# Graph values of a pair put on their diagonal by DMA; edge sums spread over feed-forward bodies; last pair with idle products and VectorE copies

## The chip, the cores and the metric

One core of one Trainium2 chip. The metric is the device time of the whole kernel in microseconds, the median of several runs: 608.84 us for the kernel before (3 runs, 607.85 to 609.2).

## What is computed

`x` has 32 sequences of 128 tokens with 128 features. Three things are done to it, in this order.

1. Attention block: layer norm, scale and shift from a condition vector, 16 heads of 64, output projection, gate, residual.
2. Feed-forward block: layer norm, scale and shift, 128 to 512, GELU, 512 to 128, gate, residual.
3. Graph block, over the 128 tokens (rows) with the first 20 tokens as keys and values. `adj` is an integer mask of 11 labels for each pair of tokens.

```
self = concat(v, q) @ W_self.T + b_self          # q is left out for rows of v that sum to 0
for d in (0, 1):                                 # two directions: adj and adj transposed
    A    = (adj or its transpose)[:, :, :20, :]
    aff  = heads(self @ Wq[d]) . heads(self[:, :20] @ Wk[d]) / sqrt(8)        # 16 heads of 8
    aff  = where(A.sum(-1) > 0, aff, -9e15) + A @ w_bias + b_bias
    w    = softmax(aff)                          # over the 20 keys
    out += heads(w @ self[:, :20], Wout[d]) + bout[d]
y = v + relu(self + out)
```

Output projection and weighting commute, so the kernel first makes `values = self[:, :20] @ Wout[d].T` (20 rows, 16 heads of 8, two directions) and then weights them.

## The kernel before, in words

The 32 sequences are 16 pairs (`PAIRS`), and each stage has one body a pair, written out for the first and last pairs and looped for the rest. All five engines run their own program and meet in semaphores; the order on each engine is the order in which its `body(s)` is written. Attention runs to about 392 us of the span, feed-forward to about 457, graph bodies to the end.

**Graph body `s`** (`graph_phase`) works on three pairs at once. For pair `s` TensorE turns the softmax weights (`turn_w`, L2070) and multiplies them with the values (`weights_v`, L2084); for pair `s+1` it makes the scores (`affinity`, L2056); for pair `s+2` it makes self features (`self_features`, L2007), turns them (`turn_self`, L2014), makes keys and queries (`keys`, L2022, whose moving operand is two runs of 20 columns; `queries`, L2031); for pair `s+3` it turns x (`turn_x`, L1999). A pair has two sequences, b = 0 and 1. TensorE's order in body `s` is:

turn_w(s,0), self_features(s+2), values(s,0), affinity(s+1,0), weights_v(s,0), turn_self(s+2), turn_w(s,1), turn_x(s+3), values(s,1), affinity(s+1,1), keys(s+2), queries(s+2), weights_v(s,1).

**Values.** 16 heads x 20 keys are 320 rows; they are split into 3 chunks of 120, 120 and 80 rows (`HC` = 6 heads, `KC` = 120 rows, `GCH` = 3). `weights_v` needs, for each chunk, a block-diagonal matrix `v_block`: head h's 20 rows hold values only in head h's 8 columns, and a ninth column of ones gives the sum of the weights. ScalarE's `copy_keys` (L2157) repeats the 20 key columns six times, so that `values` (L2044) makes 120 rows x 256 columns at once for one sequence, and VectorE's `save_v` (L2248) multiplies by a 0/1 mask `v_mask` into `v_block`. The PSUM bank (`vo_ps`) is used in turn by `values` and by the output of `weights_v`. `v_mask` is made by GpSimd at the start (L1865, L1873) and the columns of ones are set by four VectorE copies (L1885) in attention body 1 (`set_constants`).

**VectorE in body s:** bias, maximum of pair s b=1 (L2254, L2264); reciprocal and output of pair s-1 b=1 (L2275, L2280); save_v(s,0); scores minus maximum (L2268); save_self(s+2) (L2241); reciprocal and output of pair s b=0; bias, maximum of pair s+1 b=0; save_v(s,1); scores minus maximum of s+1. **ScalarE:** save_wT(s,0) (L2190, L2193), exponentials (s,1) (L2183), rectify, save_selfT(s+2) (L2150), save_wT(s,1), save_xT(s+3) (L2144), exponentials (s+1,0), save_k (L2172), save_q (L2163), copy_keys(s+2). **SP** issues the loads of x and of the q row for pair s+4 behind `self_saved` of pair s+2, the store of pair s-1, and a residual load (L1894 to L1908).

In the last body both `values` stand at its head (L2044), and 5 idle products with the identity (`multiply_identity`, L2093, `FILL` = 5, each two instructions) follow each `turn_w`.

**Feed-forward bodies** (3.6 us each): VectorE also does edge work there: `sum_labels` of the last edge block (L327) in body 3 and the three instructions of `make_bias` (L344, L346, L349) in body 10. The next pair's split (L1659) comes behind them and gates the next `hidden` products (L1490).

**Feed-forward tail:** before graph body 0, TensorE does keys and queries of pairs 0 and 1 between the last feed-forward products; ScalarE's gates (L1590) stand between the graph's copies.

## Time and profile before

| | us |
|---|---|
| median of 3 runs | 608.84 (607.85 to 609.2) |
| profiled execution | 608.95 |
| its span (first to last instruction) | 607.4 |
| granted TensorE clock | 0.998 of full speed |
| busy: TensorE / its weight loads | 594.2 / 538.0 |
| busy: VectorE / ScalarE / GpSimd | 514.0 / 466.5 / 291.1 |
| DMA | 32.55 MB, mean 54 GB/s |

The profiled execution lies 0.11 us above the median, and 1.55 us of it lie outside the span. An fp32 product is recorded as two instructions. Matmuls overlap with the weight load of the next one, so their busy times add up to more than the time they take; the chain of waits gives the time that a group really adds.

### The profile page before, as it was taken

What the parts mean: (1) busy time and instruction counts of PE and PEld (TensorE: products, weight loads), DVE (VectorE), ACT (ScalarE), POOL (GpSimd) and SP (SyncE); (2) the same over time, 40 slices, a digit from 0 to 9 for tenths busy, and PEclk for the clock granted to TensorE, in tenths of its full rate; (3) what the DMA queues carried; (4) which work ended last, traced back from release to release, by engine and by line L of the source; (5) the groups of instructions that cost most, each with busy time, mean ns of one, the idle gap of its engine ahead of it and who ended that gap; (6) DMA issues with size and microseconds to landing.
All of it is one profiled execution on the core that took longest, in us unless ns stands there. A gap on an engine that the chain in (4) does not pass through costs nothing.

```text
span 607.4 us, 17246 instructions
## 1 busy us (share of the span) xinstructions
PE 594.2 (98%) x5570; PEld 538.0 (89%) x5570; DVE 514.0 (85%) x1132; ACT 466.5 (77%) x1703; POOL 291.1 (48%) x355
## 2 busy tenths in 40 slices
PE   8999999999999999999999999999998999999996
PEld 8889999999999999999999999888887888888886
DVE  5899989888988988998998998888867878888876
ACT  4888887988889789789889879778776566566563
POOL 4445435435435435345354354556643554554551
PEclk9999999999999999999999999999999999999999
DMA  8210210210210210210201202133421212212101
GB/s 239 82 40 9 49 50 10 57 46 9 56 41 15 56 37 19 56 31 24 56 13 42 64 2 57 53 96 105 131 86 54 69 38 71 60 44 69 54 17 36
DMA packets 54678, 32.55 MB, mean 54 GB/s; under 512 B 15200, under 2 KB 52464, under 8 KB 54640
## 3 DMA queue, kind: packets, MB, share of 16 engines
q1 hardware_dynamic: 53008, 27.85, 16.9%
q0 software_dynamic: 1632, 4.21, 2.2%
q8 instruction: 21, 0.34, 0.2%
q14 instruction: 17, 0.14, 0.1%
HBM read 25.74 MB, written 6.31 MB: 53 GB/s over the span
## 4 chain that ended last, share of the span: by engine, by line
PE 88%; DVE 6%; ACT 3%; issue 1%; DMA 1%; POOL 0%; ACTq 0%; DVEq 0%; SPq 0%; POOLq 0%
PE banks L701 10%; PE banks L731 10%; PE banks L714 9%; PE banks L2084 7%; PE banks L669 5%; PE banks L673 5%; PE banks L670 5%; PE banks L2056 4%; PE banks L2070 3%; PE banks L685 2%; PE banks L754 2%; PE banks L1501 2%; PE banks L755 2%; PE banks L756 2%; PE banks L2044 2%; PE banks L2031 2%
## 5 line engine op out<-in xcount | busy, mean ns | idle before, releaser
L593 POOL TENSOR_TENSOR late_blocks<-late_blocks,p_rsum 128x512 f32<-128x512 f32 x96 | 99.0, 1052 | 156.9 <-DVE p_rsum L1076 156.9
L928 ACT ACTIVATE late_blocks<-banks,neg_max 128x128 f32<-128x128 f32 x384 | 137.1, 402 | 27.9 <-DVE neg_max L1070 27.9
L928 ACT ACTIVATION_READ_ACCUMULATOR late_blocks<-banks,neg_max 128x1 f32 x384 | 93.2, 243 | 0.0
L909 ACT ACTIVATE wide<-banks 128x512 f32<-128x512 f32 x124 | 75.6, 610 | 5.5 <-PE banks L673 4.4
L669 PE MATMUL banks<-xT_hi,w_qkv_hi 128*128 128x256 f32 x256 | 77.7, 304 | 0.0
L1070 DVE TENSOR_REDUCE neg_max<-banks 128x8 f32<-128x1024 f32 x64 | 76.5, 1195 | 1.3 <-PE banks L701 1.3
L673 PE MATMUL banks<-xT_hi,w_qkv_lo 128*128 128x256 f32 x256 | 72.2, 282 | 0.0
L670 PE MATMUL banks<-xT_lo,w_qkv_hi 128*128 128x256 f32 x256 | 71.9, 281 | 0.0
L701 PE MATMUL banks<-wide 64*128 64x128 f32 x1024 | 66.0, 278 | 0.2
L701 PEld LDWEIGHTS banks<-wide 64*128 64x128 f32 x1024 | 59.8, 188 | 6.1 <-issue 3.5
L928 ACT ACTIVATE third_p<-banks,neg_max 128x128 f32<-128x128 f32 x128 | 47.0, 387 | 20.0 <-DVE neg_max L1070 20.0
L2183 ACT ACTIVATE late_weights<-late_weights 128x640 f32<-128x640 f32 x32 | 23.6, 737 | 49.5 <-DVE late_weights L2268 49.5
L1944 POOL TENSOR_TENSOR late_blocks<-blockmask,g_kT 128x320 f32<-128x320 f32 x32 | 27.2, 870 | 57.4 <-ACT g_kT L2172 57.4
L714 PE MATMUL banks<-ident,late_blocks 128*128 128x128 f32 x384 | 50.8, 275 | 1.8 <-DVE late_weights L1083 1.2
L1094 DVE CAST oT_hi<-banks 128x512 fp32r<-128x512 f32 x62 | 42.4, 684 | 10.8 <-PE banks L731 10.6
L2084 PEld LDWEIGHTS banks<-g_v_block,g_wT 120*128 120x128 f32 (+1 forms) x384 | 46.4, 191 | 4.0 <-DVE g_v_block L2248 3.3
L669 PEld LDWEIGHTS banks<-xT_hi,w_qkv_hi 128*128 128x128 f32 x256 | 48.8, 191 | 1.1
L670 PEld LDWEIGHTS banks<-xT_lo,w_qkv_hi 128*128 128x128 f32 x256 | 48.9, 191 | 0.6
L673 PEld LDWEIGHTS banks<-xT_hi,w_qkv_lo 128*128 128x128 f32 x256 | 48.6, 190 | 0.1
L714 PEld LDWEIGHTS banks<-ident,late_blocks 128*128 128x128 f32 x384 | 42.7, 140 | 6.6 <-issue 2.2
L2084 PE MATMUL banks<-g_v_block,g_wT 120*128 120x54 f32 (+1 forms) x384 | 47.3, 274 | 0.5 <-DVE g_v_block L2248 0.5
L1099 DVE TENSOR_TENSOR oT_lo<-banks,oT_hi 128x512 fp32r<-128x512 f32 x64 | 43.9, 686 | 2.3 <-ACT oT_hi L1007 1.2
(172 smaller groups left out, 1700.7 us busy)
## 6 DMA issues: line engine op xcount, KB each, us to landing
early<-in_mask SPq DMA_DIRECT2D x16, 220.0 KB
early<-in_mask SPq DMA_DIRECT2D x80, 44.0 KB
x_in<-in_x SPq DMA_DIRECT2D x16, 128.0 KB, 2.2
...
```

The lines of the kernel that those rows point to most:

```text
L593: pool.tensor_tensor(p[:, heads, :], p[:, heads, :], p_rsum[:, b, heads].unsqueeze(2).broadcast_to([128, 4, T]), ALU.mult).then_inc(p_read ...
L669: pe.matmul(dst, g.wq_hi[:, cols], xT_hi[par][:], start=True, stop=False)
L670: pe.matmul(dst, g.wq_hi[:, cols], xT_lo[par][:], start=False, stop=False)
L673: last = pe.matmul(dst, g.wq_lo[:, cols], xT_hi[par][:], start=False, stop=True)
L701: last = pe.matmul(s_ps[b][:, e, j, :], qk[rows, c, 0, b, :], qk[rows, c, 1, b, :], start=True, stop=True)
L714: last = pe.transpose(work_ps[bank][:, m * T:m * T + T], p[:, 4 * grp + m, :], g.ident[:])
L731: last = pe.matmul(work_ps[bank][64 * e:64 * e + 64, j * T:j * T + T], v[:, b, head * DH:head * DH + DH], pT[b][:, 2 * j + e, :], start=Tr ...
L909: act.activation(qk_dst(name) if name[0] == "q" else v_dst(name), work_ps[bank], ACT.Copy).then_inc(bank_free[bank], 1)
L928: act.activation(p[:, m, :], s_ps[b][:, e, j, :], ACT.Exp, bias=neg_max[:, b, 4 * e + j:4 * e + j + 1], accum_out=p_sum[:, b, m:m + 1]).th ...
L1070: dve.tensor_reduce(out=neg_max[:, b, :].rearrange("p (e j) -> p e j", e=2), in_=s_ps[b], op=ALU.max, axis=AX.X, negate=True).then_inc(max ...
L1099: dve.tensor_tensor(oT_lo[:, 4 * half:4 * half + 4, b, :], src, oT_hi[:, 4 * half:4 * half + 4, b, :].bitcast(F32), ALU.subtract).then_inc ...
L2084: last = pe.matmul(out_ps[:, d, heads, :].rearrange("p h v -> p (h v)"), wT[0:rows, d, c, :], v_block[0:rows, s.par, b, d, heads, :].rearr ...
```

## The change

- **Values once a pair.** `values(s)` now has the 2 x 20 key columns as its stationary operand and makes 40 rows x 288 columns (`Wout` padded from 16 to 18 heads and laid out as 6 x 3). It stands for pair s+2, ahead of turn_x(s+3). ScalarE copies the keys (`kvT`, 128x40) ahead of the turned self features, and copies the values to `v_rows` (two copies of 40x144) behind save_xT(s+3); `copy_keys` and VectorE's `save_v` go.
- **Diagonal by DMA.** SP writes `v_rows` into the diagonal blocks of an image in DRAM (two transfers a pair, runs of 216 bytes), waits for them, and loads the image as `v_block` (one transfer, 311 KB). The images are cleared once in attention body 14 (two stores of 311 KB). `weights_v` waits for the load, for the output copy of the sequence before, and, for b=1, for ScalarE's copies of the values of pair s+2. Its moving operand is now six runs of 9 columns.
- **Constants.** GpSimd's mask goes. VectorE's four copies become two memsets, of 40x324 and 120x1296.
- **Edge steps.** `sum_labels` of the last block is halved over feed-forward bodies 2 and 3, the three steps of `make_bias` go to bodies 10, 11 and 12, one each.
- **Tail of feed-forward.** `values` of pairs 0 and 1 follow their `queries`; the output products of the last pair wait for the copy of the values of pair 0.
- **Last pair.** 7 idle products at the head of the last body in place of the two `values`; VectorE does the second half of the last `save_wT`.

The diff, cut:

```diff
@@ -1541,11 +1557,13 @@
         pe.wait_ge(x2_ready, PAIRS - 2)
         begin.keys(pair(0))
         begin.queries(pair(0))
+        begin.values(pair(0))
         output(pair(PAIRS - 2))
         begin.turn_x(pair(1))
         pe.wait_ge(g.edges_made, 2)
         begin.affinity(pair(0), 0)
         begin.self_features(pair(1))
+        begin.wait_values(2)
         output(pair(PAIRS - 1))
         begin.wait_keys(1)
         turn_back(pair(PAIRS - 2))
@@ -1555,6 +1573,7 @@
         begin.affinity(pair(0), 1)
         begin.keys(pair(1))
         begin.queries(pair(1))
+        begin.values(pair(1))
         pe.wait_ge(x2_ready, PAIRS)
 
...
             if more(s, 2):
                 normalise(step_from(s, 2))
             test_rows(step_from(s, -2))
-            if at(s, 3):
-                edges.parts["sum_labels"](dve, PAIRS - 1)
-            if at(s, PAIRS - 6):
-                edges.parts["make_bias"](dve)
+            for part in range(2):
+                if at(s, 2 + part):
+                    edges.parts["sum_last_labels"](dve, part)
+            for part in range(3):
+                if at(s, PAIRS - 6 + part):
+                    edges.parts["make_bias"](dve, part)
 
         if steps:
...
-                pool.affine_select(out=part, in_=part, compare_op=ALU.is_ge, fill=0.0, base=base,
-                                   pattern=[[step_h, heads], [0, GD]], channel_multiplier=mult
-                                   ).then_inc(mask_steps, 1)
-                steps += 1
-                pool.wait_ge(mask_steps, steps)
+    ROW = HC * VW
+    DIAGONAL = NG * ROW + VW
+    v_image = nc.dram_tensor("v_image", (2, 2, HC * DIAGONAL), F32, kind="Internal").ap()
+
+    def v_whole(n):
+
+        return v_image[n][:, 0:KC * ROW].rearrange("b (p e) -> p b e", e=ROW)
+
+    def v_diagonal(n, b):
+
+        blocks = v_image[n, b].rearrange("(s x) -> s x", x=DIAGONAL)[:, 0:NG * ROW]
+        return blocks.rearrange("s (m e) -> m s e", e=ROW)[:, :, 0:VW]
 
     def set_constants(dve):
         dve.wait_ge(g.kept_loaded, KEPT * 16)
-        dve.wait_ge(mask_steps, 1 + 2 * GCH)
-        for n in range(2):
-
-            for b in range(2):
-                dve.tensor_copy(v_block[:, n, b, :, :, GD],
-                                v_mask[:, :, 0].unsqueeze(1).broadcast_to([KC, 2, GH]))
+        dve.memset(v_rows[:], 1.0)
+        dve.memset(v_block[:], 0.0).then_inc(v_cleared, 1)
         dve.tensor_scalar(q_bias[:], g.gqk_b[:, 0:2], GSCALE, None, ALU.mult)
         dve.tensor_tensor(b_gsum[:], g.b_gout[:, 0:D], g.b_gout[:, D:2 * D], ALU.add).then_inc(b_gouts_added, 1)
         dve.wait_ge(b_gouts_added, 1)
         dve.tensor_tensor(b_gsum[:], b_gsum[:], g.b_self[:], ALU.add).then_inc(consts_set, 1)
 
+    def clear_images(sp):
+
+        sp.wait_ge(v_cleared, 1)
+        for n in range(2):
+            sp.dma_start(v_whole(n),
+                         v_block[:, n].rearrange("p b s d c v -> p b (s d c v)")).then_inc(v_image_cleared, 16)
+
     def sync(sp):
+        def move_values(s):
+
+            if at(s, 0):
+                sp.wait_ge(v_image_cleared, 2 * 16)
+            zero_wait(sp, v_loaded[s.par], s.half * 16)
+            sp.wait_ge(v_saved, s.n * 2 + 2)
+            for b in range(2):
+                sp.dma_start(v_diagonal(s.par, b),
+                             v_rows[b * NG:b * NG + NG].rearrange("p s d c v -> p s (d c v)")
+                             ).then_inc(v_stored[s.par], 16)
+            sp.wait_ge(v_stored[s.par], s.half * 32 + 32)
+
+            zero_wait(sp, out_full, unit_count(step_from(s, -2), 1))
+            sp.dma_start(v_block[:, s.par].rearrange("p b s d c v -> p b (s d c v)"),
+                         v_whole(s.par)).then_inc(v_loaded[s.par], 16)
+
         def load(s):
             sp.dma_start(x_in[:, s.par], g.x2_p[s.n]).then_inc(x_loaded[s.par], 16)
             sp.dma_start(q_row[:, s.par],
@@ -2032,16 +2070,11 @@
                                  selfT[:].rearrange("p b t -> p (b t)"), start=True, stop=True)
             last.then_inc(q_full, 1)
 
-        def values(s, b):
-            pe.wait_ge(kv6_ready, s.n + 1)
-
-            if at(s, PAIRS - 1) and b == 1:
-                pe.wait_ge(q_saved, PAIRS)
-            elif at(s, PAIRS - 1):
-                pe.wait_ge(shifted, unit_count(s, 0))
-            else:
-                zero_wait(pe, o_ready, unit_count(s, b) - 1)
-            pe.matmul(values_at(s, b).rearrange("p d h v -> p (d h v)"), kvT6[:, s.par, b].rearrange("p h m -> p (h m)"),
+        def values(s):
+
+            zero_wait(pe, o_ready, unit_count(step_from(s, -2), 0))
+            pe.wait_ge(kv_saved, s.n + 1)
+            pe.matmul(v_ps.rearrange("p d s c v -> p (d s c v)"), kvT[:].rearrange("p b m -> p (b m)"),
                       g.gout_w[:].rearrange("p d v -> p (d v)"), start=True, stop=True).then_inc(v_full, 1)
 
...
 
         def weights_v(s, b):
 
-            pe.wait_ge(v_saved, unit_count(s, b))
-            if at(s, PAIRS - 1):
-                pe.wait_ge(o_ready, unit_count(s, b) - 1)
+            if at(s, 0) and b == 0:
+                pe.wait_ge(v_saved, 4)
+            if b == 0:
+                pe.wait_ge(v_loaded[s.par], s.half * 16 + 16)
+            zero_wait(pe, o_ready, unit_count(s, b) - 1)
+            if b == 1 and more(s, 2):
+                pe.wait_ge(v_saved, s.n * 2 + 6)
             for d in range(2):
                 pe.wait_ge(wT_saved[d], unit_count(s, b))
                 for c in range(GCH):
                     rows = min(KC, HM - c * KC)
                     heads = slice(c * HC, c * HC + rows // NG)
...
+                pe.matmul(dst, g.ident[:], g.ident[:], start=True, stop=True)
 
         def body(s):
             here, nxt, second = more(s, 0), more(s, 1), more(s, 2)
 
             if at(s, PAIRS - 1):
-                values(s, 0)
-                values(s, 1)
+                multiply_identity(turns_ps[:, 0:T], FILL + 2)
             if here:
                 turn_w(s, 0)
             if at(s, PAIRS - 1):
-                multiply_identity()
+                multiply_identity(g.bank[0][:, 512:512 + T], FILL)
             if second:
                 self_features(step_from(s, 2))
-            if here and not at(s, PAIRS - 1):
-                values(s, 0)
             if nxt:
                 affinity(step_from(s, 1), 0)
             if here:
@@ -2116,11 +2148,11 @@
             if here:
                 turn_w(s, 1)
             if at(s, PAIRS - 1):
-                multiply_identity()
+                multiply_identity(g.bank[0][:, 512:512 + T], FILL)
+            if second:
+                values(step_from(s, 2))
             if more(s, 3):
                 turn_x(step_from(s, 3))
-            if here and not at(s, PAIRS - 1):
-                values(s, 1)
             if nxt:
                 affinity(step_from(s, 1), 1)
             if second:
@@ -2132,8 +2164,9 @@
         if steps:
             begin = Kept()
             begin.turn_x, begin.self_features, begin.turn_self = turn_x, self_features, turn_self
-            begin.keys, begin.queries, begin.affinity = keys, queries, affinity
+            begin.keys, begin.queries, begin.values, begin.affinity = keys, queries, values, affinity
             begin.wait_keys = lambda count: pe.wait_ge(k_saved, count)
+            begin.wait_values = lambda count: pe.wait_ge(v_saved, count)
...
-            zero_wait(act, kv6_ready, s.n)
+            act.activation(kvT[:], turns_ps[:, 0:2 * T].rearrange("p (b t) -> p b t", b=2)[:, :, 0:NG], ACT.Identity,
+                           bias=g.b_selfT[:]).then_inc(kv_saved, 1)
             act.activation(selfT[:].rearrange("p b t -> p (b t)"), turns_ps[:, 0:2 * T], ACT.Identity,
                            bias=g.b_selfT[:]).then_inc(selfT_saved, 1)
 
-        def copy_keys(s):
-            act.wait_ge(selfT_saved, s.n + 1)
-
-            zero_wait(act, v_full, unit_count(step_from(s, -2), 1))
-            act.activation(kvT6[:, s.par], selfT[:, :, 0:NG].unsqueeze(2).broadcast_to([128, 2, HC, NG]),
-                           ACT.Copy).then_inc(kv6_ready, 1)
+        def save_v(s):
+            act.wait_ge(v_full, s.n + 1)
+            for n in range(2):
+                zero_wait(act, v_stored[n], (s.half + (1 if n < s.par else 0)) * 32)
+            for d in range(2):
+                act.activation(v_rows[:, :, d, :, 0:GD], v_ps[:, d], ACT.Copy).then_inc(v_saved, 1)
 
         def save_q(s):
             act.wait_ge(q_full, s.n + 1)
@@ -2183,7 +2216,7 @@
             act.activation(flat, flat, ACT.Exp).then_inc(exp_done, 1)
 
         def save_wT(s, b):
-            for d in range(2):
+            for d in range(1 if at(s, PAIRS - 1) and b == 1 else 2):
                 act.wait_ge(wT_full[d], unit_count(s, b))
 
                 full_rows = HM // KC
@@ -2208,16 +2241,17 @@
                 save_wT(s, 1)
             if more(s, 3):
                 save_xT(step_from(s, 3))
+            if second:
+                save_v(step_from(s, 2))
             if nxt:
                 weights(step_from(s, 1), 0)
             if second:
                 save_k(step_from(s, 2))
                 save_q(step_from(s, 2))
-                copy_keys(step_from(s, 2))
 
         if steps:
             begin = Kept()
-            begin.save_xT, begin.save_selfT, begin.copy_keys = save_xT, save_selfT, copy_keys
+            begin.save_xT, begin.save_selfT, begin.save_v = save_xT, save_selfT, save_v
             begin.save_k, begin.save_q, begin.weights = save_k, save_q, weights
             begin.wait_constants = lambda: act.wait_ge(consts_set, 1)
...
                               r_sum[:, b].unsqueeze(3).broadcast_to([128, 2, GH, GD]),
                               ALU.mult).then_inc(o_ready, 1)
+
+        def save_last_wT(s):
+            dve.wait_ge(wT_full[1], unit_count(s, 1))
+            full_rows = HM // KC
+            rest = HM - full_rows * KC
+            dve.tensor_copy(wT[:, 1, 0:full_rows, :].rearrange("p c t -> p (c t)"), wT_ps[1][0:KC, 0:full_rows * T])
+            dve.tensor_copy(wT[0:rest, 1, full_rows, :],
+                            wT_ps[1][0:rest, full_rows * T:GCH * T]).then_inc(wT_saved[1], 1)
 
```

## Rows read from the trace of the kernel before

**Rows 1.** The page, part 4: the chain that ended last, by engine.
```profile
PE 88%; DVE 6%; ACT 3%; issue 1%; DMA 1%; POOL 0%; ACTq 0%; DVEq 0%; SPq 0%; POOLq 0%
```

**Rows 2.** The chain of waits in order of time (start us, us, what), one graph body.
```profile
543.80 0.54 PE banks L2044 x2
...
547.79 0.43 PE banks L2044 x2
...
548.97 0.57 PE banks L2022 x4
```

**Rows 3.** Timeline, same body (start us, us, engine, line; idle before, releaser).
```profile
543.08 0.53 PEld L2007 LDWEIGHTS banks<-w_self_sb,g_xT 128*128 128x128 f32 x4
543.67 0.66 PE L2044 MATMUL banks<-gout_w,g_kvT 128*120 128x256 f32 x2
544.27 0.57 PEld L2056 LDWEIGHTS banks<-late_blocks,g_qT 64*128 64x128 f32 x8 [0.34 <-issue]
545.01 1.53 PE L2084 MATMUL banks<-g_v_block,g_wT 120*128 120x54 f32 x12
546.58 0.36 DVE L2275 RECIPROCAL g_r_sum<-banks 128x32 f32<-128x32 f32 x1 [0.53 <-PE banks L2084]
546.97 0.42 DVE L2280 TENSOR_TENSOR late_outputs<-banks,g_r_sum 128x256 f32<-128x256 f32 x1
547.35 0.20 PEld L1999 LDWEIGHTS banks<-ident,g_x_in 128*128 128x128 f32 x2 [0.17 <-ACT g_selfT L2150]
547.63 0.59 PE L2044 MATMUL banks<-gout_w,g_kvT 128*120 128x256 f32 x2
548.15 0.57 PEld L2056 LDWEIGHTS banks<-late_blocks,g_qT 64*128 64x128 f32 x8 [0.34 <-issue]
551.15 0.84 ACT L2163 ACTIVATE g_qT<-banks,g_q_bias 128x256 f32<-128x256 f32 x2
552.15 0.53 PEld L2007 LDWEIGHTS banks<-w_self_sb,g_xT 128*128 128x128 f32 x4
```

**Rows 4.** Timeline: weighted values of bodies 0 and 13, first and last of 14.
```profile
462.99 1.53 PE L2084 MATMUL banks<-g_v_block,g_wT 120*128 120x54 f32 x12
...
581.39 1.53 PE L2084 MATMUL banks<-g_v_block,g_wT 120*128 120x54 f32 x12
```

**Rows 5.** Groups of instructions by line, ScalarE, 440 to 608 us.
```profile
L2172 ACT ACTIVATE g_kT<-banks,gqk_b 128x40 f32<-128x40 f32 x32 | 7.4, 282 | 2.1 <-PE banks L2022 2.1
```

**Rows 6.** Timeline, last two bodies.
```profile
588.53 0.42 DVE L2280 TENSOR_TENSOR late_outputs<-banks,g_r_sum 128x256 f32<-128x256 f32 x1
589.10 0.66 PE L2044 MATMUL banks<-gout_w,g_kvT 128*120 128x256 f32 x2 [0.32 <-DVE late_outputs L2280]
594.87 1.41 PEld L2084 LDWEIGHTS banks<-g_v_block,g_wT 120*128 120x128 f32 x12 [0.74 <-DVE g_v_block L2248]
597.83 1.28 PE L2093 MATMUL banks<-ident 128*128 128x128 f32 x10
```

**Rows 7.** Timeline, feed-forward stage: weight loads and VectorE.
```profile
406.62 0.19 PEld L1490 LDWEIGHTS banks<-f_xT_hi,w_hi 128*128 128x128 f32 x1 [0.77 <-DVE f_xT_lo L1659]
...
430.16 0.89 DVE L346 SCALAR_TENSOR_TENSOR early<-edge_sums,b_bias_sb,early 128x640 f32<-128x640 f32 x1
431.08 0.49 DVE L349 COPY edge_sums<-early 128x640 f32<-128x640 f32 x1
433.99 0.19 PEld L1490 LDWEIGHTS banks<-f_xT_hi,w_hi 128*128 128x128 f32 x1 [1.62 <-DVE f_xT_lo L1659]
439.95 0.42 DVE L1667 TENSOR_TENSOR f_x<-banks,f_x_res 128x256 f32<-128x256 f32 x1 [0.78 <-PE banks L1510]
```

**Rows 8.** Timeline, VectorE in attention body 1.
```profile
63.11 0.49 DVE L1885 COPY g_v_block<-g_v_mask 120x32 f32<-120x32 f32 x4
```

**Rows 9.** Line 731 (PE): what its engine waited for (us, times).
```profile
  DVE v L1133: 0.2, 1
```

**Rows 10.** Line 1397's transfers: time to landing.
```profile
DMA to landing us min/median/max: 2.1/2.5/4.2
```

87 lines of the change are left out of this document (43 added, 44 removed).

## Prediction, made before the changed kernel was run

> **What bounds the kernel now.** I read the page first: the chain that ended last is 88% TensorE and 6% VectorE [rows 1], so an edit counts by what it does to TensorE's order of work, and at the places where TensorE waits. Next the chain of waits in order of time, for what each group adds to a graph body, and the timeline of one body, for who has slack. Weighted values of body 0 start at 462.99 and those of body 13 at 581.39 [rows 4]: 118.40 / 13 = 9.11 us a body. Last, the places where TensorE does stand still: the feed-forward bodies and the last two graph bodies.
>
> **A. Values once a pair, bodies 0 to 13.** Before, the two `values` add 0.54 and 0.43 us to the chain [rows 2]; 0.43 for 512 streamed columns (two instructions of 256). With 288 columns each I scale to 0.48.
>
> First half of a body: `values(s,0)` goes from between self features and `affinity`. The weight load of `affinity` starts at 544.27, 0.06 before the end of the values (543.67 + 0.66) [rows 3]; the end of the self features is 543.80 (start of the values in the chain [rows 2]), so it could start at 543.74: 0.53 gained. The mask product on VectorE that followed is no gain here: the weighted values start 0.74 after `affinity`'s first load (545.01 against 544.27), while the keys, which wait for nothing, start 0.82 after theirs (548.97 against 548.15) [rows 2, 3]: TensorE's order alone held them.
>
> Second half: `values(s+2)` stands ahead of turn_x and now waits for the output copy of sequence 0, which is new at this place. That copy follows the weighted values by reciprocal and product: 546.97 + 0.42 = 547.39 [rows 3]. Where a values product waited for that copy, it started 0.15 after it (589.10, against a copy that ended at 588.53 + 0.42 = 588.95) [rows 6]. So it starts at 547.54, takes 0.59 [rows 3] + 0.05, and turn_x adds 0.22, as two one-pass products of 128 columns at 0.11 (the idle products: 1.28 for 10, less the tail of the last [rows 6]): the next weight load comes at 547.54 + 0.64 + 0.22 - 0.07 = 548.33 against 548.15 [rows 3]. Lost: 0.18. The old 0.17 wait of turn_x for `selfT` (547.35, [rows 3]) is covered by the values, also with the key copy (0.28 us by its twin in shape, [rows 5]) ahead of `selfT`. If the wait for the output copy did not bite, the loss is 0; if the turned x cannot be packed so closely, 0.35.
>
> Net 0.35 a body, times 13 from body 0 to body 13: **-4.5 us** (bounds: 0.53 x 13 = -6.9, and 0.15 x 13 = -2.0).
>
> What must keep up: the query copies end at 551.15 + 0.84 = 551.99 while the next self features load at 552.15 [rows 3]. VectorE loses `save_v` between maximum and subtraction, so the exponentials and with them the query copies come about 0.15 earlier after the output copy; TensorE reaches self features 0.18 later: 0.5 us of slack. ScalarE swaps the 6-fold key copy for a small key copy and two value copies of 40x144, about 0.3 each [rows 5]: they fall into its idle time before the exponentials. Both new waits of `weights_v` (b=1) for ScalarE and VectorE are over a microsecond old when TensorE gets there; behind them on TensorE stands only the next body.
>
> DMA: at the end of the value copies SP issues two small stores, waits, and loads the image. With at most 4.2 us for a transfer (the slowest that the feed-forward loads show [rows 10]) this is 0.8 + 4.2 + 0.4 + 4.2 = 9.6 us. From the value copies, which I put at 549.4 (the copy of x and two of 0.3 behind the turned x of 548.4), to the weighted values two bodies later (545.01 + 2 x 9.1 = 563.2) it has 13.8. Behind the waiting SP stand the loads of pair s+5's x and q rows, the store and the residual load; x is needed a body later than it is issued. ScalarE's next value copies wait for the stores of the pair before, a body (9.1) later, when 0.8 + 4.2 are over. I take nothing. Clearing the images (two stores in attention body 14) stands behind loads and ahead of an x1 store that is not due before the end of a body of attention: nothing. GpSimd made its mask before a cast that it had to wait for anyway: nothing.
>
> **B. Last two bodies.** Body 14 is not TensorE's: its second values product and weighted values waited for VectorE (0.32 and 0.74 [rows 6]). I count from the end of weights_v(13,1), old 588.11, with the old durations. turn_w(14,0) to 0.6, affinity(15,0) to 1.4, weights_v(14,0) 1.3 to 2.9 (old from 2.3: the values stood between); reciprocal and output copy to 3.7; meanwhile turn_w(14,1) to 3.55 and affinity(15,1) to 4.25; weights_v(14,1) 4.2 to 5.65 (old from 6.76 [rows 6]). VectorE: bias, maximum, subtraction of (15,0), 0.85 each, from 3.75 to 6.3, exponentials to 7.1. The 7 idle products (14 instructions x 0.11 = 1.6) fill TensorE to 7.25; turn_w(15,0) starts there, old 9.2: 1.9 earlier. turn_w(15,1) then waits 0.2 for its exponentials: 1.7 earlier. The VectorE half of the last `save_wT` (0.7 behind the output copy) ends 0.4 before the 5 idle products do, which hid ScalarE's half too: 0. **-1.7 us** (bounds -0.7, the wait of 0.74 only, and -2.5).
>
> **C. Feed-forward.** Body 3's edge sum made TensorE wait 0.77, body 10's three steps 1.62 [rows 7]. VectorE idles 0.78 in an undisturbed body before its residual [rows 7]. Half a sum (0.5) and the first step fit; the second step is 0.89 [rows 7] and sticks out by 0.1 to 0.25; the third (0.49) fits. **-2.1 us** (bounds -1.5, if the first is taken up by something else that was late behind it, and -2.4).
>
> **D. Start of the graph.** Values of pair 0 add 0.48 to TensorE's queue and delay gate, turned self features and turned x of pair 2; the key copy ahead of `selfT` adds 0.25 there, where TensorE waits for ScalarE; values of pair 1 are half covered by the wait for the queries' copy. +0.75 at body 0's self features, less 0.45 since values(0,0) is gone: **+0.3 us** (bounds 0 and +0.9).
>
> **E. Constants.** In attention body 1 VectorE has no pause from 60 to 73 us, and TensorE waits for its copy of v, once in the run, 0.2 us [rows 9]: whatever VectorE takes longer before it, TensorE loses. Removed are four copies that take 0.40 together [rows 8]. Added are 324 + 1,296 = 1,620 elements of memset, an instruction that no row shows at such a size. From below: the copy of 640 elements in 0.49 is 0.77 ns each, 1.25 us. From above: the two-source step of 640 in 0.89 is 1.39 ns each, 2.25 us [rows 7]. A memset reads nothing, so I stay near the copy, and a fifth above it, as it is the fastest of its kind here: 1.5. **+1.1 us** (bounds +0.8, +1.9).
>
> The Trainium skill, "VectorE: DVE Perf Modes", section "Zero memsets can be issued as uint32 (trn2)", says that a memset takes one cycle per element whatever the type; with its 0.96 GHz that is, as an estimate, 1.7 us for both, and the term would be +1.3. It speaks against this part of the change; no row here has such a memset.
>
> **Sum.** -4.5 - 1.7 - 2.1 + 0.3 + 1.1 = -6.9. From the profiled execution's 608.95, which is 0.11 above the median: 602.05; I say **602.1 us**.
>
> **Rivals.**
> 1. *The new wait for the output copy doesn't bite.* TensorE's own work between (turn_self, turn_w) is nearly as long as VectorE's reciprocal and product. Then 0.53 a body: 13 x 0.18 = 2.3 less, **599.8**. Against it: the modelled ends differ by 0.3.
> 2. *A slower second half or a slower follower.* turn_x, copies of keys and `selfT` and value copies queue on ScalarE; if a body gains only 0.15, 13 x 0.2 = 2.6 more, **604.7**. For it: TensorE's slack to ScalarE at the self features was 0.16 in the old body [rows 3].
> 3. *The gains are eaten up* by such queues and by the constants: **608.5**, no change to be told.
> 4. *Slower: short runs in the moving operand.* All 384 products of `weights_v` now read six runs of 9 columns. The only group that reads runs, `keys` (two of 20 columns), takes 0.57 for 4 = 0.143 each [rows 2], `weights_v` 0.105 to 0.12 with one run. If the runs are the cause, 384 x 0.037 = 14 us: 602.1 + 14.2 = **616.3**. It decides from 6.9 / 384 = 18 ns a product. Against it: 54 columns stream in 45 ns at the rate of the 256-column products (0.43 / 2), so a run could cost several times what it does and still hide under the weight load; `keys` also follows the switch from 64-row products, which leaves 0.17 idle.
> 5. *The image comes late.* The two transfers in series would have to take over 6 us each; then TensorE stands still in every body and the time is above 610. The slowest load here took 4.2 [rows 10]. It would be the part that doesn't do what it says.
>
> On 5, the loads shown move runs of 512 bytes. The Trainium skill, "DMA: Bandwidth & Descriptors", section "Specifications", says that below 512 bytes the DMA engine does a read-modify-write; the diagonal stores are runs of 216 bytes. By that rule they cost more than the loads of the same count, which is why 5 keeps a chance; no row tells how much.
>
> **Chances.** Forecast (600.8 to 603.6) 0.48; rival 1 0.15; rival 2 0.20; rival 3 0.06; rival 4 0.07; rival 5 0.04. A measurement of this kernel can tell 0.2%, about 1.2 us, from no change: faster means below 607.6. Faster 0.48 + 0.15 + 0.20 + 0.02 of rival 3 = 0.85; same 0.04; slower 0.11. The range takes in the forecast, rival 1 and most of rival 2: 599.2 to 606.3.
>
> **What would show it.** Period of the weighted values 8.76 instead of 9.11 us; the values product of a middle body starting about 0.15 behind VectorE's output copy, and nothing waiting in front of `affinity`; weight loads of `weights_v` as close as before (0.105 to 0.12); no wait for DMA at `weights_v`; image loads landing some 5 us ahead of need. In feed-forward no wait above 0.3 at the `hidden` products. In attention body 1 one wait of TensorE of 1.2 to 1.5 for the copy of v. From the start of turn_w(15,0) to the end the same 10 us as before, but for 0.2. I am wrong if the body stays above 9.0, if `weights_v` gets longer, or if ScalarE becomes what TensorE waits for.

## The result and the profile after

The changed kernel takes 603.69 us (median of 4 runs, 602.9 to 604.01) against 608.55 us for the kernel before, timed beside it (4 runs, 607.85 to 609.2). The ratio is 0.9924, 95% interval 0.9912 to 0.9936: 4.6 to 4.9 us less. The forecast was 602.1. The profiled execution took 602.9 us, span 601.3, so 6.1 us of span less than the profiled execution before. Of the difference to 4.9, 0.9 is in the start-up and 0.3 is a load that came late in one of the two, as is shown below. Of all the executions reported here, three were slow ones, all of one experiment (the image loaded twice in series: 619.78 to 621.35 us at a mean granted clock of 0.972 to 0.979), and its median leaves them out.

The chain of waits by engine, after [rows 1]:

```profile
PE 91%; DVE 5%; ACT 2%; issue 1%; DMA 0%; POOL 0%; DVEq 0%; ACTq 0%; POOLq 0%
```

I cut both traces, and those of the experiments, at the same events: first scores of attention, first turn of the feed-forward behind the last products of attention, self features of pair 0, weighted values of body 0, of body 13, and the last ones. Each stretch is the difference of two start times of weight loads in the timeline (us):

```
                      first    to feed-  to self   to body 0   to body   to last
                      scores   forward   features  w. values   13        w. values
before                13.60    378.82    53.40     17.16       118.41    20.51
changed               12.66    380.17    51.98     17.98       114.40    18.60
difference            -0.94    +1.35     -1.42     +0.82       -4.01     -1.91
forecast              0        +1.1      -2.1      +0.3        -4.5      -1.7
changed, once more    12.72    380.07    52.81     17.98       114.41    18.61
values, 128 columns   12.96    380.54    52.69     19.09       113.43    18.68
edge steps together   13.54    379.99    53.49     17.98       114.40    18.60
memsets on GpSimd     14.02    378.75    52.68     18.00       114.40    18.60
second step halved    13.07    380.06    51.65     18.00       114.40    18.60
no first idle prod.   12.60    380.08    51.62     17.99       114.39    18.55
last copy ScalarE     13.02    379.98    51.95     17.99       114.40    18.61
image twice           12.74    380.02    51.71     17.98       119.54    19.78
8 idle instructions   13.25    380.02    52.93     18.88       126.04    18.60
image beside          12.91    379.67    52.00     18.00       114.40    18.60
three mends           13.95    378.86    52.46     17.50       113.42    18.68
edge steps GpSimd     13.58    378.85    53.62     17.51       113.43    18.67
```

One middle body of the changed kernel, timeline of TensorE's weight loads (start us, us, line; idle time of the loader before them):

```profile
540.60 0.53 PEld L2045 LDWEIGHTS banks<-w_self_sb,g_xT 128*128 128x128 f32 x4
541.25 0.57 PEld L2089 LDWEIGHTS banks<-late_blocks,g_qT 64*128 64x128 f32 x8
541.99 1.42 PEld L2121 LDWEIGHTS banks<-g_v_block,g_wT 120*128 120x128 f32 x12 [0.17 <-issue]
...
544.43 0.15 PEld L2077 LDWEIGHTS banks<-gout_w,g_kvT 128*40 128x40 f32 x2 [0.26 <-DVE late_outputs L2309]
545.04 0.20 PEld L2037 LDWEIGHTS banks<-ident,g_x_in 128*128 128x128 f32 x2 [0.46 <-issue]
545.41 0.57 PEld L2089 LDWEIGHTS banks<-late_blocks,g_qT 64*128 64x128 f32 x8 [0.17 <-issue]
```

Affinity now stands 0.65 behind the self features (541.25 - 540.60) where it stood 1.19 behind them [rows 3]: the 0.54 of the first half is there in full. Affinity and weighted values are 0.74 apart, as before. In the second half the values' load waits for the output copy, and turn_x's load starts 0.61 behind the values'. From the weighted values to the next `affinity` it is now 3.42 (545.41 - 541.99), where it was 3.14 (548.15 - 545.01 [rows 3]). So this body loses 0.28 there; the bodies before lay 9.05 to 9.13 apart, and against their mean of 9.11 the loss is 0.23.

The same stretch in the chain of waits (start us, us, what), against [rows 2]; the first line is turn_x in the body before, where it stood ahead of the 0.43 of the second values:

```profile
547.44 0.35 PE banks L1999 x2
```

```profile
544.43 0.68 PE banks L2077 x2
545.11 0.37 PE banks L2037 x2
```

Values and turn_x together take 1.05 of the chain, where they took 0.78.

Feed-forward, timeline of the changed kernel, against [rows 7]:

```profile
406.74 0.19 PEld L1506 LDWEIGHTS banks<-f_xT_hi,w_hi 128*128 128x128 f32 x1 [0.30 <-DVE f_xT_lo L1678]
...
433.04 0.88 DVE L360 SCALAR_TENSOR_TENSOR early<-edge_sums,b_bias_sb,early 128x640 f32<-128x640 f32 x1
433.21 0.20 PEld L1493 LDWEIGHTS banks<-ident,f_xhat 128*128 128x128 f32 x2 [0.18 <-DVE f_xhat L1662]
434.69 0.81 ACT L1598 ACTIVATE f_xT<-banks,f_mod_cols 128x128 f32<-128x128 f32 x2 [0.56 <-DVE f_mod_cols L1668]
436.34 0.19 PEld L1506 LDWEIGHTS banks<-f_xT_hi,w_hi 128*128 128x128 f32 x1 [0.42 <-DVE f_xT_lo L1678]
```

The wait of 1.62 is gone, but the second edge step leaves a tail: VectorE's copy of the modulation columns comes late, ScalarE waits 0.56 for it, and TensorE 0.42 for what hangs on that.

The constants in attention body 1, against [rows 8, 9]:

```profile
62.30 0.33 DVE L1898 MEMSET g_v_rows<- 40x324 f32 x1
62.84 1.14 DVE L1899 MEMSET g_v_block<- 120x1296 f32 x1 [0.22 <-issue]
...
66.94 0.85 PEld L747 LDWEIGHTS banks<-second_pT,v 128*64 128x64 f32 x16 [1.37 <-DVE v L1149]
```

The last two bodies, weight loads, against [rows 4, 6]:

```profile
588.06 1.41 PEld L2121 LDWEIGHTS banks<-g_v_block,g_wT 120*128 120x128 f32 x12 [0.17 <-issue]
589.40 1.64 PEld L2128 LDWEIGHTS banks<-ident 128*128 128x128 f32 x14
590.96 0.67 PEld L2103 LDWEIGHTS banks<-ident,late_weights 128*120 128x120 f32 x6
...
595.79 1.42 PEld L2121 LDWEIGHTS banks<-g_v_block,g_wT 120*128 120x128 f32 x12
```

The waits of 0.32 and 0.74 of [rows 6] are gone. The 1.64 of idle products (L2128, x14) stands where TensorE would otherwise wait for the exponentials of the last pair, as the run without them shows below.

### The profile page after: what moved, and what is told of

It reads as the page before. It is cut to its first block, busy times and chain, and to the rows that moved or that the text cites. A ratio compares the mean times of both kernels' runs of the same rounds, so it can differ in the third digit from the quotient of the medians.

```text
span 601.3 us, 17271 instructions
## 1 busy us (share of the span) xinstructions
PE 590.1 (98%) x5552; PEld 532.0 (88%) x5552; DVE 504.3 (84%) x1101; ACT 475.4 (79%) x1733; POOL 290.1 (48%) x348
## 4 chain that ended last, share of the span: by engine, by line
PE 91%; DVE 5%; ACT 2%; issue 1%; DMA 0%; POOL 0%; DVEq 0%; ACTq 0%; POOLq 0%
PE banks L747 9%; PE banks L717 9%; PE banks L730 9%; PE banks L2121 7%; PE banks L685 5%; PE banks L689 5%; PE banks L686 5%; PE banks L1517 4%; PE banks L2089 4%; PE banks L2103 4%; PE banks L2069 2%; PE banks L770 2%; PE banks L771 2%; PE banks L772 2%; PE banks L701 2%; PE banks L703 2%
```

## The experiments

All are edits of the changed kernel (603.69; 603.22 in its second timing). The median of one and the same kernel differs by about 0.5 us from one timing to the next (the kernel before: 607.96 to 608.57), so I read a part's size from the stretches above and use the medians as a check.

**Values with a stationary operand of 128 columns**

```diff
-    kvT = sb("g_kvT", [128, 2, NG])
+    kvT = sb("g_kvT", [128, 128])
...
+        pool.memset(kvT[:, BM:128], 0.0).then_inc(kvT_filled, 1)
...
-            pe.matmul(v_ps.rearrange("p d s c v -> p (d s c v)"), kvT[:].rearrange("p b m -> p (b m)"),
+            pe.matmul(v_all, kvT[:],
```

> The values product gets a stationary operand of 128 columns in place of 40: the 88 filler columns are zeroed once by GpSimd, and the 88 extra output rows are not read. Everything else as in the changed kernel. Theory (a narrow stationary operand keeps TensorE from loading the next weights during the product, and its own during the product before): the idle time of 0.46 before the weight loads of turn_x behind the values (14 bodies), and of 0.33 and 0.46 around the two values products at the start of the graph, goes; turn_x follows the product without a gap, a middle body goes from 8.80 to 8.60 to 8.70 us, the start of the graph gains 0.5 to 0.9, the kernel 1.8 to 3.5 us (about 600 to 602 on a median of 603.7). Rival (the gap is the semaphore wait and the length of a 288-column product, whatever the operand's width): the gap stays, a body stays at 8.80, within 0.3 us of the changed kernel.

Measured: 602.68 us (6 runs), ratio to the kernel before 0.9905 (0.989 to 0.992). One body, as above:

```profile
554.97 0.30 PEld L2085 LDWEIGHTS banks<-gout_w,g_kvT 128*128 128x128 f32 x2 [0.27 <-DVE late_outputs L2317]
555.32 0.38 PEld L2043 LDWEIGHTS banks<-ident,g_x_in 128*128 128x128 f32 x2
```

The gap in the loader is gone: turn_x loads 0.35 behind the values' load, not 0.61, while the product runs. But a body gets only 0.075 us shorter (113.43 against 114.40 over 13). The theory is right about the gap, and its forecast of 0.1 to 0.2 a body was too large. The chain of waits shows why:

```profile
554.97 0.75 PE banks L2085 x2
555.73 0.22 PE banks L2043 x2
```

turn_x falls from 0.37 to 0.22, but the product takes 0.75, since its own load still waits 0.27 for the output copy and can't run ahead of it. Where nothing holds the load, at the start of the graph, the same product takes 0.48. Second values product there, with what follows it, in the changed kernel and then in the three mends (below), which have this wider operand:

```profile
460.26 0.61 PE banks L2077 x2
460.87 0.80 PE banks L2103 x6
```

```profile
460.39 0.48 PE banks L2090 x2
460.88 0.66 PE banks L2116 x6
```

So by these rows either cause by itself costs 0.27: the narrow operand 0.61 + 0.80 against 0.48 + 0.66, the held load 0.75 against 0.48 (no run takes the wait alone away; the two places are compared). Together, in the middle bodies of the changed kernel, they cost 0.35, as an estimate from these rows (0.68 + 0.37 against 0.48 + 0.22), not 0.54. So taking the narrow operand away while the load is still held gives back only 0.08 (1.05 to 0.97), and that is the 0.075.

At the start of the graph this execution was slowed by the clock (19.09 in the table, against 17.50 in the three mends with the same operand):

```profile
461.00:464.00 3.00, 3.00 (x11) 2.37 (x10) 1.76 (x3) 1.63 (x6) 2.36 (x3) 0.51 0.15 46
```

(activity by window; the third last column is the granted clock: 0.51, which is the lower of its two levels, 1.2 GHz, behind a wait of TensorE's loader of 1.61 us that ended at 458.4; in the changed kernel the same wait was followed by no fall.) A second of the six executions had the same mean granted clock (0.995, 604.54 us); the four others took 602.0 to 602.89. What the wider operand gives at that place is therefore read from the three mends: 0.48.

**Edge steps put together again**

```diff
-            for part in range(2):
-                if at(s, 2 + part):
+            if at(s, 3):
+                for part in range(2):
                     edges.parts["sum_last_labels"](dve, part)
-            for part in range(3):
-                if at(s, PAIRS - 6 + part):
+            if at(s, PAIRS - 6):
+                for part in range(3):
                     edges.parts["make_bias"](dve, part)
```

> Part C of the change undone alone: both halves of the last edge sum in feed-forward body 3 and all three edge steps in body 10, as before the change. Theory: TensorE's waits of 0.77 and 1.62 come back and those of the spread steps go, so that what the spread brings is what the traces showed between the feed-forward's start and the first self features, 1.4 us: 605.1 against 603.7. Rival (the forecast's own size): 2.1 us, 605.8. Second rival (the spread only moved the wait): within 0.3.

Measured: 604.55 us (6 runs), ratio 0.9936 (0.9919 to 0.9952). The feed-forward stretch is 53.49 against 51.98. But a wait that is nobody's edit lies in it: in the first loop body TensorE waited for nothing in four of the fourteen traces and 0.28 to 1.30 us in the others, behind VectorE, which itself waited for a load (second run of the changed kernel):

```profile
412.36 0.49 DVE L1652 BATCH_NORM_STATS2 f_stats<-f_x_in 128x6 f32<-128x128 f32 x2 [1.36 <-DMA f_x_in<-x_scratch]
```

That wait of TensorE was 0.63 before, 0.34 in the changed kernel, 0.81 here and 1.17 in the second run of the changed kernel. Without it the stretch is 52.77, 51.64, 52.68 and 51.64 (and 51.62 in the run without idle products, whose trace has no such wait). So the spread brings 1.0 to 1.1 us, and the theory's 1.4 held 0.3 of that late load.

**Second edge step in two halves**

```diff
-            for part in range(3):
+            for part in range(4):              # parts 1 and 2: a half of the second step each
```

> The second edge step (0.88 us for 640 elements) is cut in two halves, so that the four parts stand in feed-forward bodies 10 to 13. Theory (the second step sticks out of VectorE's slack of 0.78 less what its follow-ups take, and delays the copy of the modulation columns, ScalarE's f_xT and TensorE's hidden product by 0.42, and the turn by 0.18): a half of 0.45 fits, the stalls in bodies 10 to 12 of 0.8 us in all fall under 0.2, and the kernel gains 0.5 to 0.8 us. Rival: halves of 0.45 stick out as well (the last step, 0.49, still cost 0.2), then each costs 0.1 to 0.3 and the gain is under 0.3.

Measured: 602.69 us (4 runs), ratio 0.9901 (0.9886 to 0.9915). Without the late load the stretch is 51.37: 0.27 gained, the rival's size. The tail of 0.42 is gone, and each part now costs the same small wait at the turn:

```profile
433.43 0.20 PEld L1497 LDWEIGHTS banks<-ident,f_xhat 128*128 128x128 f32 x2 [0.17 <-DVE f_xhat L1666]
...
441.01 0.20 PEld L1497 LDWEIGHTS banks<-ident,f_xhat 128*128 128x128 f32 x2 [0.21 <-DVE f_xhat L1666]
```

**Memsets on GpSimd**

```diff
     def set_constants(dve):
-        dve.memset(v_rows[:], 1.0)
-        dve.memset(v_block[:], 0.0).then_inc(v_cleared, 1)
+        dve.wait_ge(v_cleared, 1)
+    # GpSimd, behind rstd_of(FIRST), where the mask was made: the same two memsets
```

> The two memsets (324 and 1,296 elements) go from VectorE in attention body 1 to GpSimd at the place where it made the mask. Theory for part E: the wait of TensorE for VectorE's copy of v in body 1 (1.37 us) falls to 0 to 0.2 and the kernel gains 1.1 to 1.4 us (602.4 on a median of 603.7); GpSimd's two memsets take 1 to 2 us there and end before its split of the weights is due at about 12 us. Rival: GpSimd's memsets take over 4 us and delay its split, on which TensorE's first products wait: no gain or a loss of up to 1 us. On the start-up: the trace of the changed kernel had TensorE's clock at full speed 1.9 us earlier than that of the kernel before and was 0.9 us ahead at 30 us. If that came from GpSimd's missing mask, this kernel starts as the one before did (first scores at about 13.6 us); if it differs from execution to execution, it may be at either.

Measured: 603.1 us (6 runs), ratio 0.991 (0.9894 to 0.9927). The stretch of attention falls from 380.1 (380.0 to 380.2, but for two traces, 379.67 and 380.54) to 378.75: 1.3 to 1.4 us gained, all of part E, and TensorE no longer waits for the copy of v. But the median gains only 0.1 to 0.6, because the start-up pays for it. Timeline of GpSimd and VectorE at the start:

```profile
5.22 0.36 POOL L1898 MEMSET g_v_rows<- 40x324 f32 x1
5.30 1.55 DVE L1064 TENSOR_SCALAR xhat<-x_in,ln_meanvar,ln_rstd 128x128 f32<-128x128 f32 x2 [0.51 <-POOL ln_rstd L602]
5.53 1.17 POOL L1899 MEMSET g_v_block<- 120x1296 f32 x1
```

and the same operation in the changed kernel:

```profile
5.12 0.60 DVE L1063 TENSOR_SCALAR xhat<-x_in,ln_meanvar,ln_rstd 128x128 f32<-128x128 f32 x2 [0.51 <-POOL ln_rstd L602]
```

VectorE's two instructions take 1.55 us instead of 0.60 and end at 6.85, 0.15 behind GpSimd's memset (6.70). The first projection of attention starts at 9.45 instead of 8.34. Neither theory nor rival had this: GpSimd wasn't slow; VectorE was slow beside it. The expectation also called a step at the start "TensorE's clock at full speed"; the granted clock is 1.00 from the first us in both traces, and that step is looked at below.

**No idle products in front of the last turn**

```diff
             if at(s, PAIRS - 1):
-                multiply_identity(turns_ps[:, 0:T], FILL + 2)
+                pass
```

> The 7 idle products in front of turn_w(15,0) are left out, the 5 behind it and the 5 behind turn_w(15,1) stay. Theory (what the last pair gained is the order: the values are no longer in the way and the exponentials come early; the idle products only fill the time until these exponentials, which end about 0.1 us before the products do): turn_w(15,0) starts at most 0.2 us earlier, the granted clock stays at its higher level to the end, and the time is within 0.3 us of the changed kernel. Rival (the idle products hold the clock up): in the 1.6 us of silence the granted clock falls to its lower level, the tail of 10 us grows by 1 to 4 us (605 to 608). Rival on the other side: the idle products themselves hold turn_w up, 0.3 to 0.5 us are gained.

Measured: 603.56 us (6 runs), ratio 0.9941 (0.9923 to 0.9959). The tail is 18.55 against 18.60, and TensorE's granted clock stays at 1.00 through the pause, from 589 to 591 us (PE busy 0.69) and behind it:

```profile
589.00:591.00 2.00, 0.69 (x6) 0.60 (x6) 1.97 (x4) 0.76 (x2) 0.00 (x0) 1.00 0.25 65
591.00:595.00 4.00, 4.00 (x38) 4.00 (x37) 2.94 (x9) 2.66 (x8) 2.19 (x3) 1.00 0.01 2
```

What TensorE does there instead is wait for the exponentials:

```profile
590.40 0.61 PEld L2103 LDWEIGHTS banks<-ident,late_weights 128*120 128x120 f32 x6 [1.43 <-ACT late_weights L2216]
```

So in this execution the idle products give nothing, and what the tail gained is the order of the work. But two of the six executions took 605.53 and 606.2 us at a mean granted clock of 0.993, in the rival's range, while the other four took 602.34 to 603.72 at 0.999, and none of the ten executions of the changed kernel was below 0.997. These two left no trace, so where their clock fell is not known; it can fall elsewhere with all the idle products in place (at 461 us above). Whether the idle products guard against it stays open.

**Last wT half back on ScalarE**

```diff
-            for d in range(1 if at(s, PAIRS - 1) and b == 1 else 2):
+            for d in range(2):                 # save_last_wT(s) on VectorE is left out
```

> The second half of the last save_wT goes back from VectorE to ScalarE, all else as in the changed kernel. Theory (forecast's 0: the 5 idle products behind turn_w(15,1) hide ScalarE's copies of both halves, which end no later than these do): within 0.3 us of the changed kernel, last weighted values at the same distance behind turn_w(15,1). Rival: ScalarE's two copies of 0.66 us in line end after the idle products (0.55 us), so the last weighted values come 0.4 to 0.8 us later.

Measured: 603.0 us (5 runs), ratio 0.9921 (0.9909 to 0.9934). Tail 18.61: nothing lost.

**Eight idle instructions where values(s,0) stood**

```diff
                 self_features(step_from(s, 2))
+            if here and second:
+                multiply_identity(g.bank[0][:, 320:320 + T], 4)
```

> Four idle one-pass products (identity by identity, 0.11 us each in the last pair's row) are put where values(s,0) stood, between the self features and affinity in bodies 0 to 13; all else as in the changed kernel. Theory (the first half of a body is TensorE's own order, nothing waits for another engine there, so what is put in or taken out counts in full): the period goes from 8.80 to 9.20 to 9.27, the kernel loses 5.5 to 6.5 us (609 to 610). Rival (a follower on VectorE or ScalarE sets the pace of a body and the product moved away was partly slack): 0 to 0.2 a body, at most 3 us lost (under 607).

Measured: 616.82 us (5 runs), ratio 1.0151 (1.0138 to 1.0164). The expectation miscounted: a product of fp32 is two instructions of 0.11, as the forecast's part B has it.

```profile
550.05 0.53 PEld L2045 LDWEIGHTS banks<-w_self_sb,g_xT 128*128 128x128 f32 x4
550.50 0.97 PEld L2128 LDWEIGHTS banks<-ident 128*128 128x128 f32 x8
551.59 0.57 PEld L2089 LDWEIGHTS banks<-late_blocks,g_qT 64*128 64x128 f32 x8
```

Put in: 8 x 0.11 = 0.88 to 0.9 us. Got: a period of 9.695 against 8.80 (126.04 / 13), 0.895. Work put in at this place counts in full, with no slack anywhere behind it; this agrees with values(s,0) giving its 0.54 in full when it was taken out.

**The image loaded twice, in series and side by side**

```diff
+            sp.dma_start(v_block..., v_whole(s.par)).then_inc(v_twice[s.par], 16)
+            sp.wait_ge(v_twice[s.par], s.half * 16 + 16)
             sp.dma_start(v_block..., v_whole(s.par)).then_inc(v_loaded[s.par], 16)
```

> SP loads each image of the values twice, the second time after the first has landed, and only the second releases the weighted values: the way from the value copies to the image is longer by one transfer with its issue and its landing (about 2.5 to 4.5 us a pair). Theory (the transfers are hidden with several us to spare; queues are not what is short): period stays 8.80, time within 0.3 us of the changed kernel, weighted values never wait for DMA. Rival (the image is close to late, or SP's other loads behind the wait are): TensorE waits in front of the weighted values of a pair or for the load of x in each body, 1 us and more a body, 615 us and more.

Measured: 610.12 us (9 runs, 607.0 to 614.94), ratio 1.0042 (1.0019 to 1.0064). The theory is wrong; the span of the profiled execution grew by 6.0 us. Timeline of SP's queue, one body:

```profile
541.95 0.40 SPq L1934 DMA_DIRECT2D g_x_in<-x_scratch  x1
...
547.26 0.32 SPq L1927 DMA_DIRECT2D g_v_block<-v_image  x1
550.41 0.32 SPq L1930 DMA_DIRECT2D g_v_block<-v_image  x1
550.99 0.41 SPq L1934 DMA_DIRECT2D g_x_in<-x_scratch  x1
```

and what SP and TensorE waited for (us in total, times, longest us):

```profile
SPq L1930 <- DMA g_v_block<-v_image: 46.9, 16, 3.2
...
PE banks L2125 <- DMA g_v_block<-v_image: 5.1, 10, 0.7
```

The chain of waits of this trace runs through SP and its transfers alone from 500 to 560 us: SP does one thing after another, 9.04 us in this body (541.95 to 550.99), of which 3.15 are the added load. TensorE's bodies follow that cycle, at 8.80 for the first two and 8.81 to 9.57 then (119.54 / 13 = 9.20 in the mean). In the changed kernel the image is far from late: it is issued here,

```profile
549.02 0.32 SPq L1926 DMA_DIRECT2D g_v_block<-v_image  x1
```

lands 3.3 us later (median of the 16), and is needed at 559.6, two bodies of 8.80 behind 541.99: 7 us to spare. Is it the queue or the bytes? The second load beside the first, into a spare tile:

```diff
             sp.dma_start(v_block..., v_whole(s.par)).then_inc(v_loaded[s.par], 16)
+            sp.dma_start(v_spare..., v_whole(s.par)).then_inc(v_loaded[s.par], 16)
```

> Each image is loaded twice as in the run that had lost time by it, but the second load goes into a spare tile and is issued right behind the first, so SP doesn't wait between them; the weighted values wait for both. It tells bandwidth from SP's order. In the other run SP's own cycle had become 9.1 us: x 0.59, q 0.67, store 0.60, residual 0.59, two image stores 0.7 and a wait of 2.2 for them, load and wait of 3.2, second load 0.6. Theory (SP as one queue that waits in line was the bound): here SP's cycle grows by 0.3 to 0.4 over the changed kernel and stays under 8.8, so period 8.80 and time within 0.4 us of it. Rival (the transfers themselves load the DMA engines so that images or x come late): weighted values wait for the image again, 0.2 us and more a body, 606 us and more.

Measured: 603.01 us (6 runs), ratio 0.9914 (0.9899 to 0.9929), period 8.80. The same bytes cost nothing; the wait in SP's line did. What SP does in a body of the changed kernel, its wait for the stores to land included, is so 9.04 - 3.15 = 5.9 us by the body shown, about 2.9 under the period of 8.80.

**The changed kernel once more, the three mends, and the edge steps on GpSimd**

> The changed kernel itself once more, beside the other three of this call. No edit. It tells how far one execution's start-up and feed-forward differ for the same program: in five traces the first scores of attention started at 12.6 to 14.0 us, and a wait for a late input in the first loop body of the feed-forward took 0.28 to 1.07 us. Theory: both belong to the execution, not to the edits; here too the stretch from the first scores to the feed-forward's first turn is 380.1 to 380.3 us and the period 8.80, while the two values above may be anything in their ranges; the time is 603.2 to 604.2. Rival (the earlier start of 0.9 us is a gain of the change, since GpSimd no longer makes a mask there): the first scores start at 12.6 to 12.8 again.

Measured: 603.22 us (6 runs), ratio 0.9916 (0.9903 to 0.993). First scores at 12.72 again. Over all traces there are two causes here. The first projection starts at 8.2 to 8.6 in every kernel without these memsets on GpSimd, the kernel before included (8.42, with GpSimd's mask beside it and VectorE's operation at its 0.60), and at 9.17 to 9.45 with them. And the first projection products stand 0.21 apart at first and then 0.11 to 0.12, as here in the kernel before (timeline, TensorE):

```profile
11.06 0.38 PE L673 MATMUL banks<-xT_hi,w_qkv_lo 128*128 128x256 f32 x1
11.27 0.28 PE L669 MATMUL banks<-xT_hi,w_qkv_hi 128*128 128x256 f32 x1
11.39 0.28 PE L670 MATMUL banks<-xT_lo,w_qkv_hi 128*128 128x256 f32 x1
```

The step came at 11.27 before and at 9.27 and 9.24 in the two traces of the changed kernel; with edits that touch nothing of the start-up it came at 8.4 to 9.0 (no idle products), at 10.57 (eight idle instructions) and at 11.21 (edge steps together), with first scores at 12.60, 13.25 and 13.54. So the time of first scores differs by 0.9 us between executions whose start-up is the same, and the early start of the changed kernel's trace needs no edit to explain it: the rival's 12.6 to 12.8 came true in this run, but not in those. There is one trace of the kernel before (13.60), just outside their range, so that no part of it is the edit's is not shown. The granted clock in the profile is 1.00 through all of it, so what makes the step stays open.

Three mends:

> Three mends together: stationary operand of the values of 128 columns, memsets on GpSimd, second edge step in two halves. Theory (the three act at different places and add up: 0.075 a body times 14 and 0.3 at the start of the graph, 1.4, and 0.3): 3.0 us under the changed kernel, 600.7 on a median of 603.7. Rival (one eats the other's gain, or the timed gains of the single runs, 1.0, 0.6 and 1.0, were partly noise of the start-up): 1.5 to 2.3 us, 601.4 to 602.2.

Measured: 601.67 us (5 runs, 601.13 to 602.38), ratio 0.989 (0.9874 to 0.9907), against 603.22 and 0.9916 for the changed kernel beside it: 1.55 us less, in the rival's range, and the fastest version here. By stretches, against the second trace of the changed kernel: attention -1.21, feed-forward -0.35, start of the graph -0.48, bodies -0.99, tail +0.07, first scores +1.23; sum -1.73. The three gains are there; without the late load (1.21 and 1.17) the feed-forward's is 0.39. The start-up takes back 1.2 of them, as VectorE waits for GpSimd's memsets again (1.66 us for the operation of 0.60). The memsets behind GpSimd's first split, or in smaller pieces, were not tried.

Edge steps on GpSimd:

```diff
             load_res(s)
+            for part in range(4):
+                if at(s, PAIRS - 6 + part):
+                    edges.parts["make_bias"](pool, part)
```

> As the kernel of the three mends, but the edge steps go from VectorE to GpSimd, behind its residual load in feed-forward bodies 10 to 13 (the addition of the bias moves from the second step to the last). GpSimd idles 1.25 to 1.57 us in such a body before it needs the moments. Theory (what VectorE pays for each part, 0.2 us of TensorE waiting for the normalised x, goes, as GpSimd has room for a part): the waits of 0.17 to 0.21 at the turn in bodies 10 to 12 fall under 0.1 and 0.3 to 0.5 us are gained over the three mends. Rival (a part of 640 elements takes GpSimd 1.5 us and more, so that its rstd comes late): each such body loses 0.3 to 0.5, the kernel is slower than the three mends by 0.3 to 1 us.

Measured: 603.04 us (6 runs), ratio 0.9919 (0.9904 to 0.9934). This is the rival, and more than its 0.3 to 1 us: 1.37 by the medians, and 2.4 in the feed-forward stretch of the traces (53.62, with no late load, against 52.46 - 1.21). GpSimd takes 2.51 and 1.94 us for the first and the last step, which VectorE does in 0.60 and 0.49 (its last step is a copy without the bias); its rstd comes late, and the turn waits:

```profile
428.97 2.51 POOL L356 TENSOR_SCALAR early<-edge_sums 128x640 f32<-128x640 f32 x1
...
434.14 0.20 PEld L1501 LDWEIGHTS banks<-ident,f_xhat 128*128 128x128 f32 x2 [1.80 <-DVE f_xhat L1670]
```

## Why the prediction was right, and where it was not

The direction and the places held, and the measured time lies in the range (599.2 to 606.3). It is 1.6 above the forecast of 602.1, just outside the forecast's own band (600.8 to 603.6), and nearer to rival 2's 604.7, though mostly for other reasons than rival 2's; the second timing of the changed kernel, 603.22, lies inside the band. (The sum itself: 6.9 off the median of 608.84 is 601.9; the 602.1 comes from the profiled execution, 0.11 above it.) By its steps:

- **A, middle bodies: -4.5 forecast, -4.0 measured.** First half 0.53 forecast, 0.54 measured, and the same place counted in full when work was put in. Second half: a loss of 0.18 forecast, 0.23 measured (0.54 less 4.01 / 13 = 0.31). That these are close is in part luck. The forecast put 0.19 on a later start (547.54 against 547.35) and nothing on the products (0.64 + 0.22 - 0.07, against 0.80 before). In the body shown the values' load starts 0.93 behind turn_w's (544.43 - 543.50), where turn_x's started 0.83 behind it (547.35 - 546.52): 0.10 later, not 0.19. And from there to `affinity`'s load it is 0.98, not 0.79. So the step that was mis-sized is the price of the products. The 0.48 and 0.22 are each what a run shows with an operand of 128 columns and no held load; a held load came with a product 0.27 longer, and the narrow operand added 0.08 to that, 1.0 us in 13 bodies. With 128 columns the term is -5.0 (118.41 - 113.42).
- **B, last two bodies: -1.7 forecast, -1.9 measured.** The order did it. VectorE's copies are worth 0 within 0.05 us, as forecast. So are the 7 idle products in the one trace without them; two untraced executions without them were about 3 us slower at a lower clock, so more than that can't be said of them.
- **C, feed-forward: -2.1 forecast; -1.0 to -1.1 measured** (the -1.42 of the trace less the late load). This is the term most mis-sized. Waits of 0.77, 0.21 and 1.62 went, 2.60 together, but 0.18 and 0.30 came in body 3's place and 0.17, 0.18, 0.42 and 0.21 in body 10's, 1.46 together. The forecast's "the second step sticks out by 0.1 to 0.25" counted one wait; VectorE's lateness reached TensorE by two ways: 0.18 at the turn and 0.42 behind ScalarE. Every part after the first costs 0.2 at the turn as well: VectorE's idle 0.78 before the residual [rows 7] is not all slack: the normalised x behind it is needed at once.
- **D, start of the graph: +0.3 forecast, +0.8 measured**, inside its bounds (0 to 0.9). From the end of the queries' loads to the next load it is 0.95 with the first values product between, not 0.48: 0.33 passes before its own load and 0.46 before the next.

```profile
448.21 0.73 PEld L2069 LDWEIGHTS banks<-g_selfT,gqk_w 128*128 128x128 f32 x4
449.28 0.15 PEld L2077 LDWEIGHTS banks<-gout_w,g_kvT 128*40 128x40 f32 x2 [0.33 <-issue]
449.89 1.59 PEld L1517 LDWEIGHTS banks<-wide,w_sb 128*128 128x128 f32 x8 [0.46 <-issue]
```

  With 128 columns both idle times go and 0.48 comes back: the product then takes the 0.48 of the forecast, and the term is 17.50 - 17.16 = +0.3. Nearly the whole miss is the narrow operand, whose price the forecast took from the streamed columns alone.
- **E, constants: +1.1 forecast, +1.3 measured.** The memsets took 0.33 and 1.14, with 0.22 between: 1.7 from start to end against the 1.5 put down. The memsets by themselves, 1.47, are what the forecast had; the gap is the miss. All of it reached TensorE, as the forecast had it from VectorE's missing pause. The Trainium skill, "VectorE: DVE Perf Modes", section "Zero memsets can be issued as uint32 (trn2)", has one cycle per element: at its 0.96 GHz 1,296 elements would be 1.35 us as an estimate; the trace has 1.14. Its total of +1.3 for the term came closer than the forecast's +1.1 by luck: 1.7 us for both memsets is what the trace has from start to end, but 0.22 of that is the gap, which neither had.

The sum of the trace without the start-up is -5.2 (1.35 - 1.42 + 0.82 - 4.01 - 1.91), and -4.9 without the late load as well; the medians have -4.9. Of the 2.0 us that the forecast had too much, C is 1.0, A and D 0.5 each and E 0.2; B gives 0.2 back. The narrow operand alone is 1.5 of it, and hides that A would otherwise have beaten its forecast by 0.5.

Rivals: 1 (the wait doesn't bite) is refuted: the values' load waits 0.26 for the output copy in every body, and with the operand of 128 columns such a held load makes the product 0.75 instead of 0.48. 2 (a slower second half or follower) is true in kind and smaller in size; of the gain a body 0.31 was left, not 0.15. 3 (no change to be told) is refuted by the ratio, 0.9936 at most. 4 (short runs in the moving operand) is refuted: twelve loads of the weighted values take 1.41 to 1.52, as before, and twelve products 1.46 and 1.26 of the chain, as before. 5 (the image late) is refuted for the kernel, but its threshold was wrong: not 6 us for each transfer, but about 2.9 us of waiting more in SP's line, by which its whole cycle passes the period. The stores with runs of 216 bytes landed 2.2 to 2.9 us after their issue in the trace of the image loaded twice, against a median of 2.2 for the loads of x with runs of 512; no run here tells what the short runs alone cost. I had set the transfer's own way against the time it has, and not added up what one queue does in a body. Of the signs named ahead, one failed: a wait of 0.42 stands at the `hidden` products, where none above 0.3 was to be.
